# Two small loads on another queue, bias sums folded to 64 partitions, and the bias products behind block 0

## What is computed

```python
def cond(x, adapter_mapping, W, b, lora_As, lora_Bs):
    A, Bm = lora_As[adapter_mapping], lora_Bs[adapter_mapping]      # (8,512,16), (8,16,512)
    return einsum('bti,oi->bto', x, W) + b + 2.0 * (x @ A @ Bm)

def ffn(x, W_base, b_base, W_router, A, B):                         # xf: 1024 x 512
    base = xf @ W_base.T + b_base
    logits = xf @ W_router.T                                        # 8 experts
    rw, sel = top_k(logits, 2); rw = softmax(rw)
    w = einsum('tk,tke->te', rw, one_hot(sel, 8))
    h = einsum('td,erd->ter', xf, A)                                # rank 16
    return base + 2.0 * einsum('ter,te,eor->to', h, w, B)

out = x + ffn(cond(x, ...), ...)
```

## Time and profile before

| | |
|---|---|
| three runs, us | 67.66, 67.83, 68.66 |
| median | 67.83 |
| the profiled execution | 67.89 |
| its span, first to last instruction | 66.1 |
| PE busy | 62.2 |
| DVE, ACT, POOL busy | 35.5, 22.2, 17.0 |
| mean granted clock of PE | 1.000 |
| moved by DMA | 10.55 MB, 160 GB/s |

### The profile page before, as it was taken

One profiled execution on the slowest core, in us unless ns is written; L12 is line 12 of the kernel. 1 busy time (PEld: TensorE's weight loads), 2 busy tenths in 40 slices (PEclk: granted clock), 3 DMA queues, 4 the chain that ended last, 5 costly groups with the idle time before them and its releaser, 6 DMA issues.

```text
span 66.1 us, 1178 instructions
## 1 busy us (share of the span) xinstructions
PE 62.2 (94%) x423; PEld 61.2 (93%) x423; DVE 35.5 (54%) x102; ACT 22.2 (34%) x46; POOL 17.0 (26%) x30
## 2 busy tenths in 40 slices
PE   5989999999999999999999999999999999999930
PEld 5979999999999999998999999999999799999920
DVE  0075299996599276115825594002768255847320
ACT  0750779508989299036103100020201131020000
POOL 6810000000999953687380000010100000000000
PEclk9999999999999999999999999999999999999999
DMA  0899997228996004246446999700044000022632
GB/s 0 255 284 382 402 391 239 78 77 192 249 379 273 0 0 107 55 108 144 109 107 224 407 311 371 270 9 0 0 159 161 7 0 0 0 105 86 223 134 87
DMA packets 5865, 10.55 MB, mean 160 GB/s; under 512 B 731, under 2 KB 2523, under 8 KB 5860
## 3 DMA queue, kind: packets, MB, share of 16 engines
q1 hardware_dynamic: 5572, 10.15, 46.4%
q10 hardware_dynamic: 288, 0.33, 1.6%
HBM read 7.37 MB, written 2.10 MB: 143 GB/s over the span
## 4 chain that ended last, share of the span: by engine, by line
PE 89%; DMA 4%; DVE 2%; issue 0%
PE ps L647 26%; PE ps L559 23%; PE ps L659 19%; PE ps L707 9%; PE ps L614 5%; DMA wt<-w_chunks 4%; PE ps L682 2%; PE ps L670 2%; PE ps L687 2%; PE ps L693 1%; PE ps L625 1%; DVE xn L512 1%; DVE wt_hi L412 0%; DVE h_stack L464 0%
## 5 line engine op out<-in xcount | busy, mean ns | idle before, releaser
L647 PE MATMUL ps<-am,x_hi 128*128 128x384 f32 x64 | 16.6, 340 | 0.0
L659 PE MATMUL ps<-bm,x_hi 128*128 128x280 f32 x64 | 12.9, 296 | 0.0
L647 PEld LDWEIGHTS ps<-am,x_hi 128*128 128x128 f32 x64 | 11.4, 188 | 0.0
L647 PE MATMUL ps<-am,x_lo 128*128 128x384 f32 x32 | 10.8, 338 | 0.0
L295 POOL TENSOR_TENSOR x_lo<-xt,x_hi 128x512 fp32r<-128x512 f32 x8 | 10.8, 1362 | 0.0
L659 PEld LDWEIGHTS ps<-bm,x_hi 128*128 128x128 f32 x64 | 10.2, 188 | 0.0
L659 PE MATMUL ps<-bm,x_lo 128*128 128x280 f32 x32 | 9.3, 292 | 0.0
L559 PE MATMUL ps<-wt_hi 128*128 128x280 f32 (+1 forms) x32 | 7.5, 334 | 0.3 <-DVE wt_hi L412 0.3
L512 DVE TENSOR_TENSOR xn<-ps,xn 128x280 f32<-128x280 f32 (+1 forms) x16 | 6.1, 419 | 2.6 <-PE ps L707 2.3
L559 PE MATMUL ps<-wt_lo,wt_hi 128*128 128x280 f32 (+1 forms) x32 | 7.3, 329 | 0.0
L402 DVE TENSOR_TENSOR wt_lo<-wt,wt_hi 128x512 fp32r<-128x512 f32 (+3 forms) x9 | 5.9, 691 | 2.0 <-ACT wt_hi L328 1.9
(11 more groups left out here) (68 smaller groups left out, 97.7 us busy)
## 6 DMA issues: line engine op xcount, KB each, us to landing
xt<-x_t SPq DMA_DIRECT2D x4, 512.0 KB, 6.5
xn<-x_n SPq DMA_DIRECT2D x4, 512.0 KB, 5.1
out_n<-xn SPq DMA_DIRECT2D x7, 256.0 KB, 2.1
wt<-w_chunks SPq DMA_DIRECT2D x3, 582.0 KB, 5.7
g_st<-g_hl SPq DMA_DIRECT2D x12, 81.0 KB, 2.1
ab<-adapters SPq DMA_DIRECT2D x8, 64.0 KB, 2.7
wt<-w_chunks SPq DMA_DIRECT2D x2, 128.0 KB, 3.0
btt<-b_t SPq DMA_DIRECT2D x1, 256.0 KB, 5.1
```

The lines of the kernel that those rows point to most:

```text
L647: last = mm(a_bank(b)[:, 0:R + WA], v[:, p, i, tok], am[:, i, level, at:at + R + WA], start=(i == 0 and n == 0), stop=False, skip_group_ch ...
L659: mm(b_bank(b)[:, 0:QB], v[:, p, i, tok], bm[:, i, level, :], start=(i == 0 and n == 0), stop=False, skip_group_check=True)
```

## The change

- The loads of idx and b_base go from SP's queue to POOL's, at its start; SP no longer waits for bsum to be cleared.
- IDLE is 29 instead of 27.
- The first 512 columns of wt_hi of chunk 1 are made by DVE (ahead of the low parts of chunk 1) and not by ACT.
- After the last bias sum DVE copies partitions 64 to 127 of bsum into partitions 0 to 63 of bfold (which lies in the space of hw); POOL adds it to bsum's first 64 partitions, between x_split(0,1) and x_split(1,0). ACT makes the high part of these 64 rows into partitions 0 to 63 of bsum_st, after G's high parts; DVE makes the low part into partitions 64 to 127, after G's low parts. Two matmuls with ones over all 128 partitions sum both.
- These matmuls, bias_row, stand between routed(0) and routed(1). The two parts of c go into a tile of their own, c_hl; ACT makes its part after x of pair 2, DVE after bt_lo. routed(2) waits for c's low parts.
- Near the end, one of the four steps of plain(4) goes ahead of stack_transpose(3), and one of plain(5) ahead of slots_routed(3).

The diff, without the lines that name the new semaphores:

```diff
 SLOTS = 32
-IDLE = 27
+IDLE = 29
 SCALING = 2.0
...
 AHEAD = 4
+HP = P // 2
 CH = D + WC
...
         bsum = sb("bsum", [P, WC])
-        bsum_hl = sb("bsum_hl", [P, 2, WC], F32R)
+        bsum_st = sb("bsum_st", [P, WC], F32R)
+        c_hl = sb("c_hl", [1, 2, WC], F32R)
...
         hw = sb("hw", [P, PAIRS, 2, P])
+        bfold = hw[0:HP].rearrange("p a t c -> p (a t c)")[:, 0:WC]
         hw_hi = sb("hw_hi", [P, NB, P], F32R)
...
                 sp.dma_start(wt[:, 0, W0_PIECES[n]], w[:, 0, W0_PIECES[n]]).then_inc(w0_in[n], 16)
-            sp.dma_start(idx_sb[:], idx).then_inc(idx_in, 16)
-            sp.dma_start(wt[:, 1, :], w[:, 1, :]).then_inc(w_in[1], 16)
-            sp.wait_ge(bsum_zero, 1)
-            sp.dma_start(bsum[0:1, :], bbase).then_inc(bbase_in, 16)
-            sp.dma_start(wt[:, 2, :], w[:, 2, :]).then_inc(w_in[2], 16)
-            sp.dma_start(wt[:, KB - 1, :], w[:, KB - 1, :]).then_inc(w_in[KB - 1], 16)
+            for k in range(1, KB):
+                sp.dma_start(wt[:, k, :], w[:, k, :]).then_inc(w_in[k], 16)
             sp.dma_start(xt[:, 0], x[:, 0]).then_inc(x_in[0], 16)
...
                         sp.dma_start(g_st[CROW + i:CROW + i + 1, :, :].bitcast(F32),
-                                     bsum_hl[0:1, i:i + 1, :].bitcast(F32).to_broadcast([1, PAIRS, WC])
+                                     c_hl[0:1, i:i + 1, :].bitcast(F32).to_broadcast([1, PAIRS, WC])
                                      ).then_inc(cst_in, 16)
...
         def _(pool):
+            pool.dma_start(idx_sb[:], idx).then_inc(idx_in, 16)
             nc.gpsimd.memset(bsum[:], 0.0).then_inc(bsum_zero, 1)
+            pool.wait_ge(bsum_zero, 1)
+            pool.dma_start(bsum[0:1, :], bbase).then_inc(bbase_in, 16)
             nc.gpsimd.memset(ident[:], 0.0).then_inc(id_zero, 1)
...
             put_adapter(1)
-            for p in range(2):
-                for n in range(2):
-                    x_split(p, n)
+            for n in range(2):
+                x_split(0, n)
+            pool.wait_ge(bfold_done, 1)
+            nc.gpsimd.tensor_tensor(bsum[0:HP], bsum[0:HP], bfold, ALU.add).then_inc(bhalf_done, 1)
+            for n in range(2):
+                x_split(1, n)
             put_adapter(2)
...
                 hi(wt_hi[:, k, D:CH], wt[:, k, D:CH]).then_inc(wc_hi_done, 1)
-                hi(wt_hi[:, k, 0:D], wt[:, k, 0:D]).then_inc(w_hi_done, 1)
+                if k > 1:
+                    hi(wt_hi[:, k, 0:D], wt[:, k, 0:D]).then_inc(w_hi_done, 1)
...
             hi(as_hl[:, :, :, 0, :], ab[:, :, 0]).then_inc(ab_hi_done, 1)
-            act.wait_ge(bsum_done, KB)
-            hi(bsum_hl[:, 0], bsum[:]).then_inc(bsum_hi_done, 1)
...
                 hi(g_hl[:, 0, c], ps[:, G_BANK + s, 0:c.stop - c.start]).then_inc(g_hi_done, 1)
+            act.wait_ge(bhalf_done, 1)
+            hi(bsum_st[0:HP], bsum[0:HP]).then_inc(bsum_hi_done, 1)
+            x_high(2)
             act.wait_ge(c_done, 1)
             for s, c in enumerate(COLS):
-                hi(bsum_hl[0:1, 0, c], ps[0:1, C_BANK + s, 0:c.stop - c.start]).then_inc(c_hi_done, 1)
-            x_high(2)
+                hi(c_hl[0:1, 0, c], ps[0:1, C_BANK + s, 0:c.stop - c.start]).then_inc(c_hi_done, 1)
             x_high(3)
...
             for k in range(1, KB):
+                if k == 1:
+                    dve.wait_ge(w_in[1], 16)
+                    nc.vector.tensor_copy(wt_hi[:, 1, 0:D], wt[:, 1, 0:D]).then_inc(w1_hi_done, 1)
                 dve.wait_ge(wc_hi_done, k + 2)
                 lo(wt_lo[:, k, D:CH], wt[:, k, D:CH], wt_hi[:, k, D:CH]).then_inc(wc_lo_done, 1)
-                dve.wait_ge(w_hi_done, k)
+                if k == 1:
+                    dve.wait_ge(w1_hi_done, 1)
+                else:
+                    dve.wait_ge(w_hi_done, k - 1)
                 lo(wt_lo[:, k, 0:D], wt[:, k, 0:D], wt_hi[:, k, 0:D]).then_inc(w_lo_done, 1)
...
             bias_sum(KB - 1)
+            dve.wait_ge(bsum_done, KB)
+            nc.vector.tensor_copy(bfold, bsum[HP:P]).then_inc(bfold_done, 1)
             dve.wait_ge(ab_hi_done, 1)
...
             for i in range(KB):
-                if i == 2:
-                    dve.wait_ge(bsum_hi_done, 1)
-                    lo(bsum_hl[:, 1], bsum[:], bsum_hl[:, 0]).then_inc(bsum_lo_done, 1)
                 dve.wait_ge(m_hi_done, 2 * i + 1)
...
                 lo(g_hl[:, 1, c], ps[:, G_BANK + s, 0:c.stop - c.start], g_hl[:, 0, c]).then_inc(g_lo_done, 1)
-            for s, c in enumerate(COLS):
-                dve.wait_ge(c_hi_done, s + 1)
-                lo(bsum_hl[0:1, 1, c], ps[0:1, C_BANK + s, 0:c.stop - c.start],
-                   bsum_hl[0:1, 0, c]).then_inc(c_lo_done, 1)
+            dve.wait_ge(bsum_hi_done, 1)
+            lo(bsum_st[HP:P], bsum[0:HP], bsum_st[0:HP]).then_inc(bsum_lo_done, 1)
             dve.wait_ge(bt_hi_done, 1)
...
                                            op0=ALU.mult, op1=ALU.subtract).then_inc(bt_lo_done, 1)
+
+            for s, c in enumerate(COLS):
+                dve.wait_ge(c_hi_done, s + 1)
+                lo(c_hl[0:1, 1, c], ps[0:1, C_BANK + s, 0:c.stop - c.start],
+                   c_hl[0:1, 0, c]).then_inc(c_lo_done, 1)
...
             for k in range(1, KB - 1):
-                pe.wait_ge(w_hi_done, k)
+                if k == 1:
+                    pe.wait_ge(w1_hi_done, 1)
+                else:
+                    pe.wait_ge(w_hi_done, k - 1)
                 pe.wait_ge(wc_hi_done, k + 2)
...
             k = KB - 1
-            pe.wait_ge(w_hi_done, KB - 1)
+            pe.wait_ge(w_hi_done, KB - 2)
             pe.wait_ge(wc_hi_done, KB + 1)
...
-            pe.wait_ge(ones_rounded, 1)
-            pe.wait_ge(bsum_hi_done, 1)
-            pe.wait_ge(bsum_lo_done, 1)
-            pe.wait_ge(m_lo_done, 4)
-            for s, c in enumerate(COLS):
-                for i in range(2):
-                    last = mm(ps[:, C_BANK + s, 0:c.stop - c.start], ones_r[:], bsum_hl[:, i, c],
-                              start=(i == 0), stop=(i == 1))
-            last.then_inc(c_done, 1)
+            def bias_row():
+
+                pe.wait_ge(ones_rounded, 1)
+                pe.wait_ge(bsum_hi_done, 1)
+                pe.wait_ge(bsum_lo_done, 1)
+                pe.wait_ge(m_lo_done, 4)
+                for s, c in enumerate(COLS):
+                    last = mm(ps[:, C_BANK + s, 0:c.stop - c.start], ones_r[:], bsum_st[:, c], start=True, stop=True)
+                last.then_inc(c_done, 1)
...
                     pe.wait_ge(g_lo_done, 2)
+                    pe.wait_ge(c_lo_done, 2)
                 if rows[0] == 0:
...
-            def plain(b):
+            def plain(b, rows=range(KB)):
...
                 p, tok = b // 2, slice((b % 2) * P, (b % 2 + 1) * P)
-                for i in range(KB):
+                for i in rows:
                     for n, (v, level) in enumerate(((x_hi, 0), (x_hi, 1), (x_lo, 0))):
...
             routed(0)
+            bias_row()
             routed(1)
...
             weighted_transpose(2)
+            plain(4, range(0, 1))
             stack_transpose(3)
-            plain(4)
+            plain(4, range(1, KB))
+            plain(5, range(0, 1))
             slots_routed(3)
-            plain(5)
+            plain(5, range(1, KB))
             slots_plain(4)
```

More of the change, by code:

```diff
@@ L167, in build @@
         w0_hi_done = sem("w0_hi_done")
+        w1_hi_done = sem("w1_hi_done")
         w_hi_done = sem("w_hi_done")
@@ L183, in build @@
         bsum_done = sem("bsum_done")
+        bfold_done = sem("bfold_done")
+        bhalf_done = sem("bhalf_done")
         bsum_hi_done = sem("bsum_hi_done")
```

## The result

| | before | changed |
|---|---|---|
| median, us | 67.98 | 70.93 |
| runs | 67.66 to 68.66 | 69.63, 70.11, 71.75, 71.77 |
| ratio, 95% interval | | 1.026 [1.0175, 1.0345] |
| span of the profiled execution | 66.1 | 67.8 (time 69.63) |
| mean granted clock of the four runs | | 1.000, 0.998, 0.976, 0.972 |

The kernel is slower, by 1.65 and 2.13 us in two of its executions and by 3.8 in the other two; the interval lies above 1 and includes 2%, so that it is slower is shown, and by more than 2% is not. I had said 68.1, and 67.2 to 69.0.

A forecast was written before the change was run, and what follows sets the result against it. PE was taken to bound the kernel, busy 62.2 of 66.1 us. Terms -0.30 + 0.8 + 0 + 0.1 - 0.34 = +0.26 on 67.89 gave 68.15, or 68.1 beside the median; range 67.2 to 69.0.

The forecast's parts named there:

- Start: Before PE's first real matmul: POOL's two DMA issues delay DVE's first cast by one 0.29 instruction, halved: +0.1 us.
- a rival with a chance of 0.1: At the start, DVE's cast is held by POOL: +0.5 instead of +0.1, 68.5 us; 69 with c late too; chance 0.1.
- Stall at the bias products: At bias_row after block 0: PE waits for DVE's low part of bsum_st, held by POOL's x_split: +0.8 us.
- the sign that I had named: At bias_row: DVE's bsum_st instruction takes over 1.2 us and ends 0.7 after a POOL x_lo.
- Bias products: After G: four PE matmuls taking 0.60 us become two, saving 0.30 us.
- tail: Near the end: plain(4) matmuls fill PE's wait for h_stack at stack_transpose(3), everything after slots_routed(3) 0.34 us earlier.
- c at slots_routed(0): At slots_routed(0): g_st copies of c land at B + 4.65, wanted at B + 4.7: 0, upper end 1.1 us.
- Constants: Before G: new DVE work, wt_hi of chunk 1 0.42 to 0.57 us and bfold 0.5 to 0.7, costs 0 by itself.
- The rival on the cast: At the start: a one-input SBUF copy may exclude GpSimd's instructions, left open, so DVE's cast is held; chance 0.1.
- Queues: DMA queues: chunks 1 to 3 and x pair 0 issued 0.3 to 0.7 us earlier, adapters no later: worth 0.
- the slow rival: Adapter loads: idx lands on POOL's queue later than about 7 us, 2.5 late, PE loses 2.1: 69.5 us; chance 0.1.
- The chance of slower: Whole kernel over 69.2 us, by the late adapters and a part of the other stalls; chance 0.1.

The follow-up runs named there:

- the two runs on fillers: Kernel before with 18 fillers instead of 27: 68.63 us, ratio 1.010; kernel before with idx and b_base loads on POOL and 40 fillers: 68.40 us, ratio 1.003.
- two traces where the start was early: Changed kernel with POOL's memsets behind DVE's casts of chunk 0: 70.39 us; changed kernel with idx and b_base loads back on SP: 71.73 us.
- with the start healed: Changed kernel with idx and b_base loads back on SP (71.73 us), or with POOL's memsets behind DVE's casts of chunk 0 (70.39 us).
- the version without stalls: Against changed kernel: loads on SP, DVE adds halves, bsum_st made ahead of G's parts, POOL pauses, c earlier, bias products in the middle of block 0: 67.00 us.
- the one of 128 rows: Changed kernel, loads back on SP, DVE's low part replaced by a 128-partition instruction, bias low part left out: ten runs, 68.5 to 73.5 us.

## Why the prediction was wrong, by its own steps

- **Start (+0.1, upper end 0.5; measured +1.81 in the profiled execution).** This is the step that failed. It had the collision of DVE's cast with POOL's memsets in it, as a rival with a chance of 0.1, and it named the h_stack memset. The bound on the delay, "at most the h_stack memset, 1.06", was nearly right: the cast was held through parts of three memsets for 1.10 in all, and PE started 0.97 late. What failed is the price of that delay. "PE works at half rate until 6.08, so 1.06 later is 0.5": this took the rise to full rate for a fixed moment. In the changed kernel it came at 9.1; that a gap puts it off, the two runs on fillers show. So the price was near twice the delay instead of half of it. And the chance was too low: POOL's last preparation ended at 3.60 and DVE's cast began at 3.64, so they had missed each other by 0.04. With two DMA issues of unknown length put ahead of that row, a collision was the likely case and not one in ten. With the start at +1.81 and the other terms as measured below (+0.6, -0.22, -0.34), the sum comes to +1.85; the trace shows +1.77.
- **Stall at the bias products (+0.8, ends 0.45 and 1.6; measured 0.6 in the profiled execution, 2.8 and 3.1 in two traces where the start was early).** That the 0.6 lies between the ends is luck: the late start had moved DVE's request behind POOL's run, so DVE took 0.83 and the sign that I had named, a held DVE instruction, was absent. The times of the chain were right to 0.2 us for DVE and to 0.5 for POOL: with the start healed, DVE asked at 24.35 to 24.55 (forecast 24.51) and POOL's x_split(1,1) ended at 25.4 to 25.5 (forecast 25.0). What failed is "it waits to 25.0 and ends about 25.7": one row had shown DVE getting in at the first end of a POOL instruction, and I made a rule of it. DVE waited for the end of POOL's run, two instructions more. I had bounded the wait by one x_lo under way; the bound was the run.
- **No fall of the clock was in the sum.** It followed from the stall of 2.9 in one kernel (3.4 us at half rate, which I estimate at 1.7 us), and not from one of 2.6 in another.
- **Bias products -0.30, tail -0.34.** In the changed kernel two matmuls take 0.38 between their first start and block 1's (27.40 to 27.78), 0.30 where PE didn't stand still before; so 0.22 and 0.30 of the 0.60 are saved. The tail's wait is gone. Both are in the 67.00 of the version without stalls, some 1.0 to 1.2 under the kernel before; the sum of the two would be 0.64, and the rest I can't place, chunk 1's high part on DVE and the rise of the clock among it.
- **c at slots_routed(0) (0).** Right: the profile shows a wait of 0.2 of PE's weight load in four of the kernels with the late bias row, the changed one among them, and the matmul after it starts less than 0.1 late.
- **Constants (0).** Right. The cast of 512 columns took 0.43 and the copy bfold 0.49, the lower of the two prices each time. The rival on the cast had left open whether such a cast and POOL's instructions exclude each other; memsets held it, as shown above.
- **Queues (0).** ("A second earlier" in the prediction should read a microsecond.) idx landed at 4.7 us instead of 4.4, so the slow rival fell; SP waited 1.2 for it, and the adapters were complete at 15.8 instead of 15.0, without effect on PE.
- **The chance of slower (0.1)** stood on late adapters alone. The real mechanism stood in the list with a price a third of its size.

## What to carry to other kernels

When an instruction is put ahead of POOL's or DVE's at the start, look at which instruction of the other engine will now fall on the same microseconds, and take as the bound of its delay the whole unbroken run of POOL, not the instruction under way; a semaphore wait that makes POOL pause at the right place took 4.0 us off here. A gap of PE ahead of its real work has a price of its own beside the delay: 0.97 late behind a gap of 1.02 cost 1.81, while with the gap filled a start as late cost about 0.15 between the medians. So let the fillers reach to the real start, and keep POOL's memsets away from the first casts in DVE. Moving work behind a stage moves its preparation too: keep the preparation where it was, ahead of the stage, and move only the product.

## What the runs showed of the hardware

- A DVE cast of 128x256 in SBUF, one input, was held by POOL memsets, which read nothing: 0.29 alone, 0.74, 1.07 and 1.39 beside them. With the memsets behind the casts it took 0.29 again, though the DMA issues stayed on POOL.
- A DVE instruction with two SBUF inputs, 0.83 alone, took 3.03 and 3.33 us when it was kept out until the end of three POOL instructions; in the trace of the kernel before (1.33) and in the one of 128 rows (1.36) it got in after the first.
- PE's granted clock fell to 0.50 for 3.4 us after PE had been idle for 2.94 us in the middle of dense work (it fell less than one us after work had begun again), and in another kernel it didn't fall after 2.65 us of idle time.
- POOL took 0.68 and 0.52 us to issue a DMA, SP 0.34 and 0.28; idx landed 3.5 us after the start of its issue on POOL, and SP first read it 2.7 after the start of the issue on SP.
